# A two-number read of every eighth row of x, issued by ScalarE ahead of the conditions

## The chip, the core and the metric

One NeuronCore of one Trainium2 chip runs the whole kernel. The metric is the device time of one execution in microseconds (us). The kernel before takes 46.37 us, the median of 3 runs (46.32 to 46.39).

## The reference

x is float32, 64 samples of 64 channels by 512 positions. Each sample has a condition, an index into a table of 200 matrices of 64 by 64. The result adds to each sample its own product with its matrix:

```python
w = weights[conditions]
return x + jnp.einsum('bct,bcd->bdt', x, w)
```

The kernel adds the identity to each matrix, so that one product gives the sum of both terms.

## The kernel before

Two samples make a pair: 128 partitions (2 samples of 64 channels), 32 pairs, 512 positions. x in HBM is laid out as [128, 32, 512], so one row of it is 64 KB and every eighth row is 512 KB further on. The work goes in 8 turns of four pairs each (`TURNS`), 1 MB of x and 1 MB of output a turn.

SP (`on_sync`) issues the eight loads of x (L85) without a wait; each has a semaphore of its own. It then waits for the load of turn 6 (L87), and from there issues one store a turn (L91), each after ScalarE and VectorE have both copied their half of the turn out of PSUM; the last turn's store is cut in two (L95). At the end it waits for all stores (L96).

ScalarE (`on_scalar`) first issues the load of the conditions, 64 numbers, one row (L99). Its first work then loads an activation table and zeroes the corners of `w_diag` (L102). After that it waits for `w_ready`, copies matrices into the diagonal blocks of `w_diag` (L107) and the first half of each turn's products into `y_sb` (L111, L116).

VectorE (`on_vector`) waits for the conditions, computes two table rows for each condition (L161), which TensorE spreads over the 128 partitions with small matmuls (L130); VectorE turns them into integers (L164). GpSimd (`on_gpsimd`) then issues the indirect gather of 128 table rows of 8 KB, 1 MB in all (L122). When they have landed VectorE adds the identity (L170), transposes blocks of 32 by 32 (L173) and so makes `w_all` ready. It then copies matrices (L179) and the second half of each turn's products (L182, L186).

TensorE (`on_tensor`) waits for `w_ready`. In turns 0 to 3 it multiplies each sample of a pair by itself with 64 by 64 tiles (L147), in turns 4 to 7 a pair at a time with the 128 by 128 block-diagonal `w_diag` (L143). Two sets of PSUM tiles let a turn run while the one before is copied out.

Each queue is in program order. The order around the change is thus written by hand: SP's queue holds the loads of x, ScalarE's the conditions, GpSimd's the gather. All of these transfers are carried by the same 16 DMA engines. In the profile, queue q1 is SP's, q10 is ScalarE's and q0 GpSimd's.

Of the kernel before, what the change touches and what calls it, by code (L numbers as in the profile page):

```python
# [7 lines left out]
def conditioned_residual_kernel(nc: bass.Bass, x: bass.AP, conditions: bass.AP, table: bass.AP, out: bass.AP):  # L8
# [10 lines left out]
    fp32 = mybir.dt.float32  # L19
# [3 lines left out]
    P, PAIRS, T = x.shape  # L23
# [9 lines left out]
    with ctx:  # L33
        def sbuf(name, shape, dtype):
            return ctx.enter_context(nc.sbuf_tensor(name, shape, dtype))

        def semaphore(name):
            return ctx.enter_context(nc.semaphore(name))

        x_sb = sbuf("x_sb", [P, PAIRS, T], fp32)  # L40
        y_sb = sbuf("y_sb", [P, PAIRS, T], fp32)
        condition = sbuf("condition", [1, PAIR, Q], i32)

        row_along = sbuf("row_along", [1, PAIR, K, Q], fp32)
# [11 lines left out]
                   for s in range(SETS)]  # L56

        x_loaded = [semaphore(f"x_loaded{turn}") for turn in range(TURNS)]
        condition_loaded = semaphore("condition_loaded")
        one_set = semaphore("one_set")  # L60
        zero_set = semaphore("zero_set")
# [12 lines left out]
        def halves(h):  # L74
            return slice(h * C, (h + 1) * C)

        def pairs_of(turn):
            return slice(4 * turn, 4 * turn + 4)

        def round_of(turn, j):  # L80
            return slice(4 * turn + 2 * j, 4 * turn + 2 * j + 2)

        def on_sync(sp):
            for turn in range(TURNS):
                sp.dma_start(x_sb[:, pairs_of(turn), :], x[:, pairs_of(turn), :]).then_inc(x_loaded[turn], 16)  # L85

            sp.wait_ge(x_loaded[LAST - 1], 16)  # L87
            for turn in range(LAST):
                sp.wait_ge(moved_by_act, turn + 1)
                sp.wait_ge(moved_by_dve, turn + 1)  # L90
                sp.dma_start(out[:, pairs_of(turn), :], y_sb[:, pairs_of(turn), :]).then_inc(stored, 16)  # L91
            for j in range(2):
                sp.wait_ge(moved_by_act, TURNS + j)
                sp.wait_ge(moved_by_dve, TURNS + j)
                sp.dma_start(out[:, round_of(LAST, j), :], y_sb[:, round_of(LAST, j), :]).then_inc(stored, 16)  # L95
            sp.wait_ge(stored, 16 * (TURNS + 1))  # L96

        def on_scalar(act):
            act.dma_start(condition[:, :, :], conditions).then_inc(condition_loaded, 16)  # L99
            act.wait_ge(zero_set, 1)  # L100
            for h in range(PAIR):
                nc.scalar.copy(w_diag[halves(h), :, (1 - h) * D:(2 - h) * D],  # L102
                               zero[halves(h), :].unsqueeze(2).to_broadcast([C, PAIRS - 4 * TILED, D]))
            act.wait_ge(w_ready, 1)
            for turn in range(TURNS):
                if turn < TILED:
                    nc.scalar.copy(w_diag[halves(0), pairs_of(turn), 0:D],  # L107
                                   w_all[halves(0), :, pairs_of(TILED + turn)].rearrange("p d n -> p n d"))
                if turn < LAST:
                    act.wait_ge(multiplied, turn + 1)  # L110
                    nc.scalar.copy(y_sb[:, 4 * turn:4 * turn + 2, :], product[turn % SETS][0][:, :, :]  # L111
                                   ).then_inc(moved_by_act, 1)

            for j in range(2):
                act.wait_ge(multiplied, TURNS + j)
                nc.scalar.copy(y_sb[:, 4 * LAST + 2 * j, :], product[LAST % SETS][j][:, 0, :]).then_inc(moved_by_act, 1)  # L116
# [36 lines left out]
        def on_vector(dve):  # L153
# [30 lines left out]
            for j in range(2):  # L184
                dve.wait_ge(multiplied, TURNS + j)
                nc.vector.tensor_copy(y_sb[:, 4 * LAST + 2 * j + 1, :], product[LAST % SETS][j][:, 1, :]  # L186
                                      ).then_inc(moved_by_dve, 1)

        on_sync(nc.sync)
        on_scalar(nc.scalar)  # L190
        on_gpsimd(nc.gpsimd)
        on_tensor(nc.tensor)
# [30 lines left out]
```

## Time and profile before

| | before |
|---|---|
| median of 3 runs | 46.37 us |
| the profiled execution | 46.28 us |
| its span, first to last instruction | 45.0 us |
| HBM read, written | 9.44 MB, 8.39 MB |
| mean rate over the span | 396 GB/s |
| TensorE busy | 23.1 us |
| VectorE, ScalarE, GpSimd busy | 14.9, 13.9, 1.6 us |
| granted TensorE clock, mean | 0.977 of full speed |

All times in the rows count from the start of the span. The profiled execution is 1.28 us longer than its span, which is what lies around the first and last instruction. "Share" of the DMA is the mean busy share of the 16 engines; in narrow windows a packet counts where it starts, so shares over 1 occur there. Issuing a transfer is done by a queue (ACTq, SPq, POOLq) and doesn't count as busy time of the engine.

### The profile page before, as it was taken

To read this page: it belongs to the slowest core of one execution; us is meant where nothing else is said; L and a number is where in the kernel's file an instruction comes from. 1 tells how busy PE (TensorE), PEld (TensorE's weight loads), DVE (VectorE), ACT (ScalarE), POOL (GpSimd) and SP (SyncE) were. 2 spreads that over 40 slices of the span, in tenths; PEclk is the share of its full clock that TensorE was granted. 3 is DMA by queue.
4 is the path that set the end of the run, shared out by engine and by line. 5 is a ranking of instruction groups with operands and counts; after the bars stand their busy time and mean duration, and the time that the engine had idled before them with its cause. 6 is when DMAs were issued, how large, how long until landed. Compare 5 with 4: busy or idle time off the path is not lost.

```text
span 45.0 us, 294 instructions
## 1 busy us (share of the span) xinstructions
PE 23.1 (51%) x98; PEld 9.9 (22%) x98; DVE 14.9 (33%) x24; ACT 13.9 (31%) x16; POOL 1.6 (4%) x9
## 2 busy tenths in 40 slices
PE   0040000000000079999999999999999999200000
PEld 0040000000000034243463453443544433000000
DVE  1310000000019940069999900820720753600000
ACT  0899100000000050068988800800710733500000
POOL 4009000000000000000000000000000000000000
PEclk9999999999999999999999999999999999999955
DMA  0679999999999999999999999999999999999993
GB/s 0 124 299 423 423 423 430 430 423 437 423 423 430 430 423 437 423 423 430 408 437 423 423 437 423 415 444 415 423 437 415 430 430 423 423 430 426 383 415 146
DMA packets 2594, 17.83 MB, mean 396 GB/s; under 512 B 290, under 2 KB 290, under 8 KB 546
## 3 DMA queue, kind: packets, MB, share of 16 engines
q1 hardware_dynamic: 2448, 16.78, 89.9%
q0 software_dynamic: 144, 1.05, 5.5%
q10 hardware_dynamic: 2, 0.00, 0.0%
HBM read 9.44 MB, written 8.39 MB: 396 GB/s over the span
## 4 chain that ended last, share of the span: by engine, by line
PE 51%; DMA 24%; DVE 8%; issue 2%; DVEq 0%
PE product L143 31%; DMA gathered<-weights,table_row 22%; PE product L147 19%; DVE w_all L173 5%; DMA condition<-conditions 3%; DVE y_sb L186 2%; PE product L130 1%; DVE row_along L161 1%; DVE gathered L170 1%; DVE table_row L164 0%; DVEq L167 0%
## 5 line engine op out<-in xcount | busy, mean ns | idle before, releaser
L147 PE MATMUL product<-x_sb,w_all 64*64 64x512 f32 x64 | 8.6, 696 | 13.0 <-DVE w_all L173 13.0
L143 PE MATMUL product<-x_sb,w_diag 128*128 128x512 f32 x32 | 14.0, 595 | 0.0
L182 DVE COPY y_sb<-product 128x1024 f32<-128x1024 f32 x7 | 8.6, 1224 | 10.2 <-PE product L143 6.8
L111 ACT COPY y_sb<-product 128x1024 f32<-128x1024 f32 x7 | 7.1, 1012 | 10.9 <-PE product L143 7.4
L143 PEld LDWEIGHTS product<-x_sb,w_diag 128*128 128x128 f32 x32 | 6.0, 190 | 7.9 <-issue 7.9
L147 PEld LDWEIGHTS product<-x_sb,w_all 64*64 64x64 f32 x64 | 3.4, 206 | 17.5 <-DVE w_all L173 13.1
L107 ACT COPY w_diag<-w_all 64x256 f32<-64x256 f32 x4 | 2.6, 639 | 11.3 <-DVE w_all L173 11.3
L170 DVE TENSOR_TENSOR gathered<-gathered,piece 128x64 f32<-128x64 f32 x1 | 0.3, 268 | 10.2 <-DMA gathered<-weights,table_row 10.2
L173 DVE STREAM_TRANSPOSE w_all<-gathered 128x2048 f32<-128x2048 f32 x1 | 2.3, 2312 | 0.0
L102 ACT COPY w_diag<-zero 64x1024 f32<-64x1024 f32 x2 | 2.1, 1042 | 0.0
L186 DVE COPY y_sb<-product 128x512 f32<-128x512 f32 x2 | 1.4, 691 | 1.5 <-PE product L143 1.5
L130 PE MATMUL product<-one,row_along 1*128 1x1 f32 x2 | 0.6, 344 | 2.4 <-DVE row_along L161 2.4
L116 ACT COPY y_sb<-product 128x512 f32<-128x512 f32 x2 | 1.2, 585 | 1.8 <-PE product L143 1.8
L102 ACT ACT_TABLE_LOAD x1 | 1.3, 1283 | 1.3 <-PEq L201 1.3
L179 DVE COPY w_diag<-w_all 64x256 f32<-64x256 f32 x4 | 1.6, 400 | 0.1
L122 POOL DMA_INDIRECT gathered<-weights,table_row x1 | 1.1, 1068 | 2.1 <-DVE table_row L164 2.1
L130 PEld LDWEIGHTS product<-one,row_along 1*128 1x128 f32 x2 | 0.5, 308 | 2.4 <-issue 2.4
L161 DVE TENSOR_SCALAR row_along<-condition 1x64 f32<-1x64 int32 x2 | 0.3, 179 | 0.7 <-DMA condition<-conditions 0.7
L164 DVE CAST table_row<-product 128x1 int32<-128x1 f32 x1 | 0.2, 159 | 0.7 <-PE product L130 0.7
L120 POOL MEMSET piece<- 32x1 f32 x4 | 0.4, 91 | 0.5 <-POOLq L201 0.3
L154 DVE MEMSET zero<- 128x1 f32 x1 | 0.1, 59 | 0.8 <-PEq L201 0.8
L157 DVE MEMSET piece<- 32x1 f32 x4 | 0.2, 59 | 0.2
(5 smaller groups left out, 0.5 us busy)
## 6 DMA issues: line engine op xcount, KB each, us to landing
x_sb<-x SPq DMA_DIRECT2D x8, 1024.0 KB, 14.2
out<-y_sb SPq DMA_DIRECT2D x7, 1024.0 KB, 7.0
out<-y_sb SPq DMA_DIRECT2D x2, 512.0 KB, 5.8
condition<-conditions ACTq DMA_DIRECT2D x1, 0.2 KB
gathered<-weights,table_row POOLq DMA_INDIRECT x1, 9.8
```

The lines of the kernel that those rows point to most:

```text
L102: nc.scalar.copy(w_diag[halves(h), :, (1 - h) * D:(2 - h) * D], zero[halves(h), :].unsqueeze(2).to_broadcast([C, PAIRS - 4 * TILED, D]))
L107: nc.scalar.copy(w_diag[halves(0), pairs_of(turn), 0:D], w_all[halves(0), :, pairs_of(TILED + turn)].rearrange("p d n -> p n d"))
L111: nc.scalar.copy(y_sb[:, 4 * turn:4 * turn + 2, :], product[turn % SETS][0][:, :, :]).then_inc(moved_by_act, 1)
L116: nc.scalar.copy(y_sb[:, 4 * LAST + 2 * j, :], product[LAST % SETS][j][:, 0, :]).then_inc(moved_by_act, 1)
L122: nc.gpsimd.indirect_dma_start(gathered[:, :], None, table, bass.IndirectOffsetOnAxis(ap=table_row[:, 0:1], axis=0)).then_inc(w_gathered, 16)
L130: nc.tensor.matmul(product[0][0][:, 0, 0:1], row_along[:, :, :, :].rearrange("one h k n -> one (h k n)"), one[:, :], start=True, stop=True ...
L143: product_of = nc.tensor.matmul(product[turn % SETS][j][:, g, :], w_diag[:, n - 4 * TILED, :], x_sb[:, n, :], start=True, stop=True)
L147: product_of = nc.tensor.matmul(product[turn % SETS][h][halves(g), j, :], w_all[halves(h), :, n], x_sb[halves(h), n, :], start=True, stop= ...
L173: nc.vector.transpose(w_all[:, :, :], gathered[:, :].rearrange("p (d c) -> p d c", d=D)).then_inc(w_ready, 1)
L179: nc.vector.tensor_copy(w_diag[halves(1), pairs_of(turn), D:PAIR * D], w_all[halves(1), :, pairs_of(TILED + turn)].rearrange("p d n -> p n ...
L182: nc.vector.tensor_copy(y_sb[:, 4 * turn + 2:4 * turn + 4, :], product[turn % SETS][1][:, :, :]).then_inc(moved_by_dve, 1)
L186: nc.vector.tensor_copy(y_sb[:, 4 * LAST + 2 * j + 1, :], product[LAST % SETS][j][:, 1, :]).then_inc(moved_by_dve, 1)
```

## The change

A scratch of 16 partitions with two float32 numbers each is added. ScalarE's first instruction becomes a transfer of elements 0 and 1 of rows 0, 8, 16, ... 120 of x into it, 16 rows of 8 bytes; the load of the conditions follows on the same queue. SP waits for this transfer at its very end, after the last store is issued. Nothing reads the scratch.

```diff
+        touched = sbuf("touched", [P // 8, 1, 2], fp32)
...
+        rows_touched = semaphore("rows_touched")
...
                 sp.dma_start(out[:, round_of(LAST, j), :], y_sb[:, round_of(LAST, j), :]).then_inc(stored, 16)
+            sp.wait_ge(rows_touched, 16)
             sp.wait_ge(stored, 16 * (TURNS + 1))

         def on_scalar(act):
+
+            act.dma_start(touched[:, :, :], x.rearrange("(r e) n t -> r e n t", e=8)[:, 0, 0:1, 0:2]
+                          ).then_inc(rows_touched, 16)
             act.dma_start(condition[:, :, :], conditions).then_inc(condition_loaded, 16)
             act.wait_ge(zero_set, 1)
```

## Rows read from the trace of the kernel before

**Rows 1.** The page, part 2: tenths of busy time in 40 slices of the span.

```profile
PE   0040000000000079999999999999999999200000
...
DMA  0679999999999999999999999999999999999993
GB/s 0 124 299 423 423 423 430 430 423 437 423 423 430 430 423 437 423 423 430 408 437 423 423 437 423 415 444 415 423 437 415 430 430 423 423 430 426 383 415 146
```

**Rows 2.** The chain that ended last, in order of time: start, duration, what.

```profile
0.75 1.18 DMA condition<-conditions
...
1.96 0.30 DVE row_along L161 x2
...
2.39 0.57 PE product L130 x2
...
2.98 0.17 DVE table_row L164
...
3.42 9.78 DMA gathered<-weights,table_row
...
13.61 2.32 DVE w_all L173
...
15.97 8.63 PE product L147 x63
24.61 13.95 PE product L143 x32
...
38.58 0.69 DVE y_sb L186
```

**Rows 3.** Windows: stretch, its length, five engines busy, clock, DMA share, GB/s.

```profile
4.80:7.20 2.40, 0.00 (x0) 0.00 (x0) 0.00 (x0) 0.00 (x0) 0.00 (x0) 1.00 1.03 430
...
13.20:22.91 9.71, 6.94 (x52) 2.90 (x56) 6.22 (x7) 3.73 (x5) 0.00 (x0) 1.00 1.02 428
22.91:24.40 1.49, 1.49 (x16) 0.52 (x11) 1.43 (x2) 1.46 (x2) 0.00 (x0) 1.00 1.02 423
...
24.40:36.40 12.00, 12.00 (x32) 5.40 (x29) 5.11 (x5) 4.14 (x5) 0.00 (x0) 1.00 1.01 425
...
39.20:44.50 5.30, 0.00 (x0) 0.00 (x0) 0.07 (x1) 0.00 (x0) 0.00 (x0) 0.85 0.96 396
```

**Rows 4.** Timeline of the issuing queues, single issues: start, duration.

```profile
0.75 0.49 ACTq L99 DMA_DIRECT2D condition<-conditions  x1
...
0.76 0.38 SPq L85 DMA_DIRECT2D x_sb<-x  x1
...
1.19 0.43 SPq L85 DMA_DIRECT2D x_sb<-x  x1
...
33.01 0.33 SPq L91 DMA_DIRECT2D out<-y_sb  x1
...
36.44 0.33 SPq L91 DMA_DIRECT2D out<-y_sb  x1
...
37.62 2.05 SPq L95 DMA_DIRECT2D out<-y_sb  x2
...
39.34 0.33 SPq L95 DMA_DIRECT2D out<-y_sb  x1
```

**Rows 5.** The start: queues in 1.6:1.7, then in 1.7:1.8, then three windows.

```profile
q10 hardware_dynamic: 2, 0.00, 1.5%
...
q1 hardware_dynamic: 4, 0.03, 203.9%
...
1.78:4.80 3.02, 0.55 (x2) 0.50 (x2) 0.45 (x3) 2.86 (x3) 1.07 (x1) 1.00 0.98 355
...
2.20:2.40 0.20, 0.01 (x1) 0.04 (x1) 0.04 (x1) 0.20 (x1) 0.00 (x0) 1.00 0.15 41
2.40:2.60 0.20, 0.20 (x2) 0.20 (x2) 0.00 (x0) 0.19 (x2) 0.00 (x0) 1.00 0.31 123
```

**Rows 6.** Timeline of ScalarE up to 16 us.

```profile
1.28 1.28 ACT L102 ACT_TABLE_LOAD   x1 [1.28 <-PEq L201]
...
2.57 2.10 ACT L102 COPY w_diag<-zero 64x1024 f32<-64x1024 f32 x2
...
15.95 0.63 ACT L107 COPY w_diag<-w_all 64x256 f32<-64x256 f32 x1 [11.29 <-DVE w_all L173]
```

**Rows 7.** Waits of SP's queue: total us, times, longest.

```profile
SPq L96 <- DMA out<-y_sb: 5.3, 1, 5.3
```

**Rows 8.** Timeline of GpSimd, its indirect transfer.

```profile
3.42 1.07 POOL L122 DMA_INDIRECT gathered<-weights,table_row  x1 [2.15 <-DVE table_row L164]
```

**Rows 9.** DMA queues in 4.5:7.7, then 7.7:10, then 10:12.3: packets, MB, share.

```profile
q1 hardware_dynamic: 196, 1.34, 100.6%
...
q0 software_dynamic: 63, 0.52, 52.9%
q1 hardware_dynamic: 60, 0.49, 50.4%
...
q0 software_dynamic: 66, 0.53, 54.6%
q1 hardware_dynamic: 69, 0.44, 45.7%
```

## The prediction, made before the changed kernel was run

> **What bounds the kernel now.** I read the page first. The DMA engines are 9 tenths busy from the third slice to the last but one, and move 423 to 437 GB/s in nearly all of them [rows 1]; TensorE is busy for only 23 of 45 us. The chain of waits nevertheless runs through the conditions, the gather and TensorE, because the profile follows the last store back to the copy that released it [rows 2]. So two limits run side by side, and the question is which has room. From 4.8 us on the transfers go at 425 to 430 GB/s without a hole, and the last 5.30 us of them move 396 x 5.30 = 2.10 MB [rows 3], which is exactly the last two stores' worth (1 MB of turn 6, twice 0.5 MB of turn 7). So turn 6's store begins to flow at 39.2 us. It was issued at 36.44 [rows 4]. An issue needs 1.02 us to its first packet: x's first transfer is issued at 0.76, and its queue q1 is first seen moving in 1.70 to 1.80, at about 1.78 [rows 4, 5]. Its packets could have started at 37.46, so they waited 39.20 - 37.46 = 1.74 us behind older stores. Of the other stores, turn 5's was issued at 33.01 and takes 2.46 us to flow (1.05 MB at 425 GB/s), so it has 39.20 - 2.46 - 34.03 = 2.7 us of room, and turn 7's two have 39.20 + 2.46 - (37.62 + 1.02) = 3.0 and, for the last, 42.9 - (39.34 + 1.02) = 2.5 us. Turn 6 is the tightest: **everything from the conditions to the copies may slip by 1.74 us before a DMA engine runs dry; each further us is a us of time.** Conversely the only things that shorten the run are fewer bytes or an earlier or fuller start of the transfers.
>
> The start is not full: from 1.78 to 4.80 us only 355 GB/s x 3.02 us = 1.07 MB move [rows 5], which at 430 GB/s takes 2.49 us. So 0.53 us are lost there, nearly all before 2.8, where the engines show 41 to 123 GB/s in 2.2 to 2.6 [rows 5].
>
> **The change, part by part.**
>
> *The added issue on ScalarE.* The conditions' issue takes 0.49 us on ACT's queue, and SP's issues of the same form 0.38 to 0.43 when seen singly [rows 4, 6]. The touch is taken at 0.49, so the conditions are issued at 1.24 instead of 0.75. ACT's table load and its two fills of w_diag move along by 0.49, from an end at 4.67 to 5.16; w_all frees ACT's next copy only at 15.95, and 10.8 us of idle time cover it [rows 6]. Without that cover it would cost its 0.49.
>
> *The transfer itself.* It has 16 rows of 8 bytes, so some 16 data packets and up to 16 completions. The conditions' two packets filled 1.5% of 16 engines for 0.1 us, that is 24 ns on one engine [rows 5]. One such pair on each engine is 24 ns, ahead of x in time that is idle anyway: 0, or 0.02 if it comes into x's way.
>
> *The wait at SP's end.* The touch has landed long before; behind it stands only the wait for the stores, 5.3 us long [rows 7]. Cost 0; uncovered, one semaphore check, for which no row has a duration.
>
> *x's loads.* SP issues its first at the same moment as ACT (0.76 against 0.75), so they move past nothing in program order. The conditions' packets came at 1.6 to 1.7, x's first at 1.78 [rows 5]: ACT's first transfer is about 0.14 us ahead. If the slow start is the price of a first access to x's rows, the touch pays it 0.14 us earlier. Bounds: 0 (start unrelated, or the touch's packets no faster than x's own), 0.14 if x's packets still wait for the same accesses, 0.53 if 8 bytes open a region so much faster that nothing is left; below nothing -0.1 if both issues share what makes descriptors (SP's issues grew from 0.38 to 0.43 beside it). I take 0.1.
>
> *The conditions' landing, which is the term that matters.* They now reach the engines after x's packets instead of before them. Their issue ends at 1.24 + 0.49 = 1.73; before, it ended at 1.24 and the packet came at 1.64, 0.4 later. Lower bound: served at once, at 2.13, a delay of 0.49. Upper bound from the nearest row, the only transfer of another queue that is set behind x's: the gather's issue ends at 3.42 + 1.07 = 4.49 [rows 8], and up to 7.70 its queue q0 moves nothing, while q1 is 100% busy [rows 9]. That is 3.2 us, so the conditions' packet would come at 4.93, a delay of 3.3. In that wait are also steps of GpSimd's software queue, which ACT's has not. What the wait is for x's packets: at 1.73 each engine holds the eight packets that x's first transfer gives it (1,024 KB in 8 KB packets over 16 engines), and these are through at 4.80. If the conditions get in only ahead of the last one, they come at 4.80 - 0.31 (8 KB at 26.7 GB/s, a sixteenth of 427) = 4.49, and the delay is 4.49 - 1.64 = 2.85. I take 2.85: it is nearer to the gather's row than to an empty engine. All that follows is a chain with no slack of its own: two row_along, the matmuls, table_row, the gather, the diagonal, the transpose, PE at 15.97 [rows 2]. The gather keeps its 9.8 us, since q0 and q1 share alike once it flows (63 and 60 packets to 10.0 us, 66 and 69 after [rows 9]) and x's loads still flow then. PE starts at 18.8, the stores come 2.85 later, and 2.85 - 1.74 = 1.11 us reach the end.
>
> In that last stretch the rows show the two queues alternating in small steps. The Trainium skill (DMA: Bandwidth & Descriptors, Queues, rings and completion order) says that an engine drains a whole packet of several descriptors from one row's ring before it turns to the next, typically 9 to 17. By that rule the conditions wait for all eight of x's, +3.2 and an end at about 47.8; the equal counts in both halves of the gather do not show such blocks, so the sum above does not use it.
>
> **Sum.** Against the profiled execution's own 46.28 us (span 45.0 and 1.28 around it; 0.09 under the median of 46.37): +1.11 - 0.1 = +1.0, thus 47.3, and 47.4 against the median. What a measurement of this kernel can tell from no change is about 0.2%, 0.09 us.
>
> **Rivals.**
> A. *Hidden, no change.* The conditions get in between x's first packets (delay 0.5 to 1.7, under the room of 1.74) and the slow start stays as it is. For it: the packet-by-packet sharing [rows 9]. Against: the 3.2 us. Time 46.3 to 46.45.
> B. *Faster.* The conditions are as quick as in A, and the touch opens x's regions. 46.37 - 0.14 to 46.37 - 0.53: 45.85 to 46.25, about 46.15. For it: the slow first packets are seen only at the start; the first stores after 22.9, to an output not yet touched, show no dip (428 and 423 GB/s [rows 3]), which speaks against a first-access price for every region.
> C. *The conditions wait for x's second transfer too*, issued at 1.19 and so ahead of them: it is through at about 7.2, a delay of 5.5, +3.8, 50.1. For it: the gather began only as x's second transfer was through.
> D. *The change does nothing it says*: x opens its own rows 0.14 us behind and the start is as slow, as in A, but with the conditions late: the forecast without its 0.1, 47.5; it is in the forecast.
> The point of decision between forecast and A is a delay of 1.74 us, four or five of x's packets on one engine.
>
> **Chances.** Forecast (slower, delay 1.8 to 3.3, with or without the 0.1): 0.47. A 0.18, B 0.29, C 0.04; a small loss of 0.1 to 0.3 us with quick conditions, from an x start that the touch pushes back, 0.02. Slower 0.53, same 0.18, faster 0.29. Both signs hold much of it: the forecast's own range is 46.6 (delay 2.0) to 48.0 (3.3 and no gain). The range reaches down into B, to 46.0, and up to 48.1.
>
> **What would show it.** Conditions: the wait of row_along ends at 4.8 instead of 1.96 (2.5 to 3.6 in A or B). PE's first product at 18.8; turn 6's store issued at 39.3; a hole of about 1 us in the DMA share before it. In 1.78 to 4.80 the rate stays near 355 GB/s; in B it rises over 390. The forecast is wrong if row_along starts before 3.7, or if the transfers show no hole and the span shrinks.

## The result, and the profile after

The changed kernel takes 48.55 us (median of 6 runs, 47.96 to 51.16) against 46.34 us for the kernel before beside it: a ratio of 1.041, 95% interval 1.035 to 1.046. The ratios here compare only runs in the faster of two states, into which executions of either kernel fall; of these six that leaves four, with a median of 48.26 us against 46.32. It is slower, as forecast, but by 1.9 us (2.2 in the profiled pair) where 1.0 was said, and above the range, which ended at 48.1. The profiled execution took 48.45 us, its span 47.2 us, against 46.28 and 45.0.

Part 2 of the page, the kernel after, 40 slices of the span:

```profile
PE   0000040000000000099999999999999999992000
...
DMA  0679999999999999999981999999999999689995
GB/s 0 118 320 424 424 424 424 424 438 424 431 417 438 410 438 424 410 424 424 431 341 42 403 445 431 389 403 445 438 389 417 424 445 403 264 341 438 382 414 205
```

Against [rows 1] the row of the DMA engines has two new holes: one at slice 22 (42 GB/s), where before the first store already flowed, and one at slices 35 and 36 (264 and 341 GB/s), ahead of turn 6's store. The first three slices, where the touch was to help, have not become fuller (118 and 320 GB/s, before 124 and 299).

The chain that ended last, kernel after: start, duration, what.

```profile
1.19 4.21 DMA condition<-conditions
...
5.42 0.29 DVE row_along L168 x2
...
6.88 10.45 DMA gathered<-weights,table_row
...
17.73 2.32 DVE w_all L180
...
20.10 8.74 PE product L154 x58
28.84 13.95 PE product L150 x32
...
42.81 0.69 DVE y_sb L193
```

Line by line against [rows 2]: the conditions are issued 0.44 us later (1.19 against 0.75), but row_along starts 3.46 us later (5.42 against 1.96). The gather takes 10.45 us instead of 9.78, another 0.67. PE starts 4.13 us later, and the last copy 4.23 us later.

DMA queues of the kernel after, in 1.7:2.15, then in 2.15:3.6, then in 4.8:4.9 (packets, MB, share of 16 engines):

```profile
q1 hardware_dynamic: 13, 0.11, 142.3%
...
q1 hardware_dynamic: 52, 0.43, 77.3%
q10 hardware_dynamic: 32, 0.00, 1.2%
...
q1 hardware_dynamic: 10, 0.05, 132.1%
q10 hardware_dynamic: 2, 0.00, 1.7%
```

ScalarE's q10 has 34 packets now: 32 of the touch and 2 of the conditions. The touch was not ahead of x at all: 13 packets of x started by 2.15 us, and the touch's 32 came only after that. The conditions' two came in 4.8 to 4.9, where x's first load is through, instead of 1.6 to 1.7 [rows 5].

Windows of the kernel after (as [rows 3]), and the first store and turn 6's store in the timeline of SP's queue:

```profile
1.78:4.80 3.02, 0.00 (x0) 0.00 (x0) 0.00 (x0) 3.00 (x3) 0.00 (x0) 1.00 0.99 347
24.64:25.90 1.26, 1.26 (x16) 0.63 (x12) 1.18 (x3) 1.09 (x3) 0.00 (x0) 1.00 0.02 7
...
40.68:41.70 1.02, 1.02 (x3) 0.38 (x2) 0.60 (x1) 0.59 (x1) 0.00 (x0) 1.00 0.47 193
...
25.06 0.35 SPq L94 DMA_DIRECT2D out<-y_sb  x1
...
40.68 0.33 SPq L94 DMA_DIRECT2D out<-y_sb  x1
```

The start moves 347 GB/s, before 355 [rows 5]: nothing was opened. The engines stand still for 1.26 us after the last load, because turn 0's copies are not yet there (VectorE's ends at 24.96, the store is issued at 25.06, before at 22.91). Turn 6's store is issued at 40.68 instead of 36.44, and in the 1.02 us until its packets can start the engines move only 193 GB/s.

### The profile page after: what moved, and what is told of

Its sections match the earlier page's. It is cut to its first block, busy times and chain, and to the rows that moved or that the text cites. A ratio compares the mean times of both kernels' runs of the same rounds, so it can differ in the third digit from the quotient of the medians.

```text
span 47.2 us, 295 instructions
## 1 busy us (share of the span) xinstructions
PE 23.2 (49%) x98; PEld 10.0 (21%) x98; DVE 14.9 (32%) x24; ACT 13.8 (29%) x16; POOL 1.7 (4%) x9
## 4 chain that ended last, share of the span: by engine, by line
PE 49%; DMA 31%; DVE 8%; issue 1%; ACTq 1%; DVEq 0%
PE product L150 30%; DMA gathered<-weights,table_row 22%; PE product L154 19%; DMA condition<-conditions 9%; DVE w_all L180 5%; DVE y_sb L193 1%; PE product L137 1%; ACTq L104 1%; DVE row_along L168 1%; DVE gathered L177 1%; DVE table_row L171 0%; DVEq L174 0%
## 6 DMA issues: line engine op xcount, KB each, us to landing
gathered<-weights,table_row POOLq DMA_INDIRECT x1, 10.5
```

## Experiments

The columns of windows and queues in this section are those already explained. On the four chips used for these runs the time around the span lay anywhere between 1.3 and 2.4 us, for the kernel before too; so spans are compared beside the times. All readings of packets and starts come from one profiled execution of each kernel.

**The touch behind the conditions.**

```diff
-            act.dma_start(touched[:, :, :], ...).then_inc(rows_touched, 16)
             act.dma_start(condition[:, :, :], conditions).then_inc(condition_loaded, 16)
+            act.dma_start(touched[:, :, :], ...).then_inc(rows_touched, 16)
```

> The touch follows the conditions on ScalarE's queue; nothing else differs from the changed kernel. Theory (all the loss is the conditions falling behind x's first eight packets on their engine): the conditions land at 1.9 us as before, row_along starts at 1.96, PE at 16.0, and the time is that of before, 46.3 us within 0.2. Rival 1 (the touch itself costs transfer time, or upsets x's first transfer): some of the 2.2 us stay, 46.8 or more. Rival 2 (the touch opens x's rows and the start becomes fuller): under 46.2.

row_along started at 1.98 and PE at 15.92, as before: the conditions' lateness is gone with the order of the two transfers. The times, 46.27 to 47.59 against 46.72 to 47.30, could not tell half a us, so the same kernel was timed again:

> The kernel with the touch behind the conditions once more, in more rounds, since its first comparison did not resolve 0.5 us. Theory (the touch costs and gives nothing by itself): within 0.2 us of the kernel before. Rival 1: slower by 0.3 us or more, from a touch that stands behind x's first load. Rival 2: faster.

Ratio 1.0014, interval 0.9991 to 1.0038; the spans behind it were 45.0 to 45.3 against 44.9 to 45.2. The touch by itself costs nothing that can be measured, and gives nothing. ScalarE's queue in 4.9:5.8, the profile of this second timing:

```profile
q10 hardware_dynamic: 30, 0.00, 1.8%
```

Issued right behind the conditions, 30 of its 32 packets came in this stretch and the last two by 6.5, all of them after x's first load was through: here it is the touch that waits, and nobody waits for it.

**Another first transfer.** The touch is replaced by a read of the 256 bytes of the conditions themselves into a scratch of that size; the rest is the same.

```diff
-            act.dma_start(touched[:, :, :], x...[:, 0, 0:1, 0:2]).then_inc(rows_touched, 16)
+            act.dma_start(touched[:, :, :], conditions).then_inc(rows_touched, 16)
```

> In place of the touch ScalarE first reads the conditions into a scratch, one row, 256 bytes, and reads nothing of x. Theory (an issue of about 0.45 us ahead is enough, whatever it reads): the second read lands at 4.8 to 5.4, PE starts at 19.5 to 20.3 and the time is 47.8 to 48.6. Rival (the 16 small packets of the touch or their rows of x are what holds the conditions up): the conditions land at 2.3 to 2.6, 0.45 late, and the time is 46.3.

Ratio 1.039 (1.030 to 1.049). The conditions' packets came in 4.9 to 5.0, row_along started at 5.47 and PE at 19.98. Three of the four times (48.44 to 49.16) lie above the forecast's 48.6, on a chip where the kernel before took 46.72 to 47.30; the spans were 46.8 to 47.9 against 44.9 to 45.1. It makes no difference what is read, nor in how many packets.

**No first transfer, only the lateness.** The kernel before with one wait:

```diff
+            act.wait_ge(pieces_set, 2 * (P // Q))
             act.dma_start(condition[:, :, :], conditions).then_inc(condition_loaded, 16)
```

> The kernel before, with one wait ahead of the conditions' issue (for the eight pieces, set at 1.28 us), so they are issued at about 1.3 instead of 0.75, and no transfer stands ahead of them. Theory (a late issue alone does it): packet at 4.8 to 5.2, behind x's first eight, row_along at 5.3 to 5.6, time 48.0 to 48.6. Rival (it needs another transfer ahead on ScalarE's queue): packet at 2.2, time as before.

The chain that ended last, this kernel:

```profile
1.31 4.00 DMA condition<-conditions
...
5.33 0.29 DVE row_along L162 x2
...
6.79 10.33 DMA gathered<-weights,table_row
```

The same 4 us from issue to landing, with nothing ahead on ScalarE's queue. The fastest of its four runs took 48.33 us, span 47.0 (the kernel before beside it 44.8 to 45.0 in all runs but one of 46.2). The step that costs is the late issue beside x's loads, and nothing of the touch.

**Later still.** A memset of 1,024 columns on VectorE, with a semaphore that ScalarE waits for ahead of the conditions:

```diff
+            act.wait_ge(filled, 1)
             act.dma_start(condition[:, :, :], conditions).then_inc(condition_loaded, 16)
...
+            nc.vector.memset(unused[:, :], 0.0).then_inc(filled, 1)
```

> The same, with the issue held by a memset of 1,024 columns on VectorE, to about 1.9 to 2.4 us, when three of x's loads are issued. If the wait is for what an engine has read ahead, about eight packets: packet 0.9 + 2.5 us after the start of the issue, 5.3 to 5.8. If it is for every load issued ahead: x's second is through at 7.2 and its third at 9.7, so the packet comes at 7.2 or later.

The issue started at 2.50 us, later than meant. The queues in 0:6.3, then in 6.3:6.4, this kernel, and the start of row_along:

```profile
q1 hardware_dynamic: 225, 1.71, 71.4%
...
q1 hardware_dynamic: 10, 0.08, 193.1%
q10 hardware_dynamic: 1, 0.00, 1.1%
...
7.01 0.29 DVE row_along L165 x2
```

The packet came 3.8 to 3.9 us after the issue began. That is 2.9 to 3.0 more than the 0.9 of an empty engine (0.75 to 1.64), or nine to ten packets of 0.31; the forecast said eight. x's second load was issued more than a us before. Of the 2.10 MB of its first two loads 1.71 MB had begun when the packet came, so the second was not waited for to its end. So the wait isn't for all loads issued ahead. It has the length of eight to ten of x's packets; that the engine has read these ahead is the reading that fits, and no row shows it directly.

**Issued behind the fill of w_diag in program order.**

```diff
-            act.dma_start(condition[:, :, :], conditions).then_inc(condition_loaded, 16)
...
+                if h == 0:
+                    act.dma_start(condition[:, :, :], conditions).then_inc(condition_loaded, 16)
```

> The kernel before, with the conditions issued after ScalarE's first fill of w_diag, at 3.1 us instead of 0.75, so that they reach the engines at about 4.0 in the middle of x's first load, with six more loads issued. If an engine has read ahead some eight packets of whatever queue: packet at 4.0 + 8 x 0.31 = 6.5, row_along at 6.9. If it is every load issued ahead of it: x's first three or four, 9.6 us or more. If the queues simply alternate and the wait of the changed kernel belongs to the start alone: 4.4. The time follows from row_along's lateness less 1.74: 6.5 gives 4.9 - 1.74 = 3.2 more.

This missed its aim: the issue did not wait for the fill. It began while the table load was running, only 0.17 us late. Timeline of this kernel:

```profile
0.75 1.28 ACT L101 ACT_TABLE_LOAD   x1 [0.75 <-PEq L202]
...
0.92 0.49 ACTq L104 DMA_DIRECT2D condition<-conditions  x1
...
3.50 0.28 DVE L162 TENSOR_SCALAR row_along<-condition 1x64 f32<-1x64 int32 x2 [2.23 <-DMA condition<-conditions]
```

It gives a point in between: 0.17 us late in the issue, packet in 2.8 to 2.9, row_along 1.54 us late. The span stayed at 45.0 in the profile, as the room of 1.74 us has it (45.6 in the other run); the times (46.88 and 47.37) resolve nothing. The question that it was to answer, a late issue in the middle of the stream, is answered by the run with the memset alone.

**x's first load in two halves.** The changed kernel with eight packets of 4 KB an engine first:

```diff
-                sp.dma_start(x_sb[:, pairs_of(turn), :], x[:, pairs_of(turn), :]).then_inc(x_loaded[turn], 16)
+                for pairs in ([slice(0, 2), slice(2, 4)] if turn == 0 else [pairs_of(turn)]):
+                    sp.dma_start(x_sb[:, pairs, :], x[:, pairs, :]).then_inc(x_loaded[turn], 16)
...
-                pe.wait_ge(x_loaded[turn], 16)
+                pe.wait_ge(x_loaded[turn], 32 if turn == 0 else 16)
```

> The changed kernel with x's first load cut in two of 512 KB, so that each engine gets eight packets of 4 KB (1.2 us of transfer) before the second half's eight. Theory by whole load (the conditions wait until the load issued ahead of them is through on their engine, and the second half is issued at the same time as they are): packet at 3.5 to 3.8 instead of 5.0, row_along at 3.9 to 4.2, end 1.2 us earlier, 47.0 to 47.3. Rival (they wait for a fixed number of bytes, or until the queue is read in some 3 us): row_along still at 5.2 to 5.5, time 48.3.

The conditions' packets came in 3.7 to 3.8, row_along at 4.30. Half the bytes ahead of them, and they are 1.1 us earlier: the wait is for x's packets, and for a number of them rather than of bytes, since these are eight again, of half the size. One run took 47.06 us, span 45.8, as forecast; the other, the profiled one, 48.89 and 47.6.

**The gather on empty engines.** The kernel before, with x's loads from the second on held until the gather has landed.

```diff
+                if turn == 1:
+                    sp.wait_ge(w_gathered, 16)
                 sp.dma_start(x_sb[:, pairs_of(turn), :], x[:, pairs_of(turn), :]).then_inc(x_loaded[turn], 16)
```

> The kernel before, with x's loads from the second on held until the gather has landed: the gather meets engines that are idle from 4.8 us on. It measures the gather's 3.2 us between the end of its issue (4.49) and its first packet. If the wait is for x's packets that the engines had read ahead: first packet at 5.0 to 5.5, and the gather through 2.5 us later, landing at 8.0. If it is the software queue's own latency: first packet at 7.7 as before, landing at 10.5. The total time is longer by the lost transfer time and is not what is asked.

Queues in 4.5:5.1, then in 5.1:5.3, this kernel:

```profile
q1 hardware_dynamic: 25, 0.09, 36.7%
...
q0 software_dynamic: 8, 0.07, 256.8%
q1 hardware_dynamic: 2, 0.00, 0.6%
```

The gather's first packet came at about 5.2, 0.7 us after its issue's end, and not at 7.7. Of the 3.2 us that the prediction read in [rows 9], 2.5 were x's packets ahead, eight of them, and 0.7 its own way. Landing was at 9.1, not 8.0, so that its 1 MB takes 3.9 us even alone, where 2.5 were expected; part of this is a slow start.

This run also shows two more starts on engines that stood still: the gather's at 5.18, and x's second load's at 10.09, after 1.2 us without a packet. Their first 3.02 us, this kernel, and beside them the first us of the stores in the changed kernel, which begin at 25.90 on engines that stood still as well:

```profile
5.18:8.20 3.02, 0.00 (x0) 0.00 (x0) 0.00 (x0) 0.00 (x0) 0.00 (x0) 1.00 0.99 320
10.09:13.11 3.02, 1.22 (x8) 0.59 (x12) 2.13 (x2) 0.63 (x1) 0.00 (x0) 1.00 1.02 345
...
25.90:26.90 1.00, 1.00 (x12) 0.36 (x8) 0.97 (x2) 1.00 (x2) 0.00 (x0) 1.00 1.08 451
```

Both starts of reads are as slow as x's first (355 GB/s [rows 5]), and the start of the stores isn't. In the kernel before the same second load of x follows the first without a break and runs at 430 GB/s [rows 3]. So the slow start belongs to reads that begin on idle engines, three times of three here, and not to the first access to x.

**The touch really ahead.** SP's loads are held until 1.3 us, in the kernel before and in the changed one.

```diff
         def on_sync(sp):
+            sp.wait_ge(pieces_set, 2 * (P // Q))
             for turn in range(TURNS):
```

> The kernel before, with SP's loads held for 0.55 us by a wait for the pieces. Control for the next one. x's first packet at 2.3; every later transfer 0.55 later, time 46.9. Theory of the slow start (first packets of all engines at once are slow, whenever they come): the first 3 us of transfer still lose 0.5 us.

> The changed kernel with the same hold: the touch is now some 0.6 us ahead of x's first packets, and the conditions (issued at 1.2) come ahead of them too, at 2.1. Theory: no conditions' wait for x, PE 0.45 later than before (16.4), time as x_held, 46.9. Rival (touching opens x's rows where it really comes first): x's first packets take 0.31 us instead of 0.4 to 1.0 and the time is up to 0.5 us under x_held, 46.4.

The first 3.02 us of x's transfers, first without, then with the touch:

```profile
2.32:5.34 3.02, 0.55 (x2) 0.50 (x2) 0.16 (x1) 2.31 (x3) 1.07 (x1) 1.00 0.97 353
```

```profile
2.31:5.33 3.02, 0.55 (x2) 0.49 (x2) 0.44 (x3) 2.77 (x3) 1.07 (x1) 1.00 0.98 339
```

All 32 packets of the touch lay in 1.7 to 2.0 here, 0.3 us or more ahead of x's first at 2.3. x's start moved 339 GB/s, without it 353: rows touched beforehand are not read faster. The spans, 45.7 with the touch and 45.4 to 45.7 without, say the same, and so do the times: 47.0 and 46.7 to 47.0 us, as forecast for no effect. With the hold the conditions came ahead of x again and row_along started at 2.43.

**The room, measured by itself.** The kernel before with an additional transpose of the gathered rows into a scratch, of 1,024 and of 2,560 columns; nothing changes at the start.

```diff
             dve.wait_ge(identity_added, 1)
+            nc.vector.transpose(unused[:, 0:1024], gathered[:, 0:1024])
```

The version with 2,560 columns has two such lines, of 2,048 and of 512.

> The kernel before, with one more transpose of 1,024 columns on VectorE (half of the 2.31 us one, 1.16 us) between the identity and the real transpose: everything from w_all on comes 1.16 us later and no transfer at the start changes. Theory (there are 1.74 us of room before turn 6's store): time within 0.2 of before. Rival (there is no room, PE's chain sets the end): +1.16.

> The same with 2,560 columns, 2.9 us later. Theory: +2.9 - 1.74 = +1.15, a hole of about 1.1 us in the transfers ahead of turn 6's store. Rival (no room): +2.9. Rival (the loss comes from the reordering of the transfers at the start, not from PE's lateness): +0.

With 1,024 columns PE started at 17.27, 1.30 late, and the ratio is 1.0003 (0.9955 to 1.0050); the transfers show no hole:

```profile
24.00:41.00 17.00, 16.65 (x60) 7.00 (x52) 8.47 (x10) 7.36 (x10) 0.00 (x0) 1.00 1.01 424
```

With 2,560 columns PE started at 18.73, 2.76 late, and the hole ahead of turn 6's store is there, with the start of the transfers unchanged:

```profile
40.30:41.50 1.20, 1.20 (x4) 0.57 (x3) 0.71 (x2) 0.50 (x2) 0.00 (x0) 1.00 0.24 96
```

Its spans were 45.8, 46.6, 46.7 and 47.1, that is 0.8 to 2.1 over 45.0 where 1.0 follows from 2.76 - 1.74. The profiled execution explains its own: TensorE's first 64 products took 10.08 us (8.63 before), so the last copy began 4.19 late. Over the profiled executions, by the start of the last copy (before: 38.58):

| kernel | last copy late | less 1.74 | span over 45.0 |
|---|---|---|---|
| conditions behind the fill | 1.60 | 0 | 0.0 |
| 1,024 columns | 2.11 | 0.37 | 0.2 |
| x's first load in two | 2.77 | 1.03 | 2.6 (other run 0.8) |
| conditions twice | 3.92 | 2.18 | 1.8 |
| 2,560 columns | 4.19 | 2.45 | 2.1 |
| the change | 4.23 | 2.49 | 2.2 |
| conditions waited | 4.46 | 2.72 | 3.3 (other run 2.0) |
| conditions late | 6.08 | 4.34 | 4.0 |

Two profiled executions stand out above the line, and another run of each (0.8 and 2.0) does not. The others lie at the forecast or 0.2 to 0.4 under it, so the room is nearer 2.0 than 1.74 us. The last copy's lateness holds more than the delay put in: TensorE's first 64 products took 8.6 to 10.1 us over these runs, with the same work, for a reason that no run isolates. With the touch second (second timing) the last copy was 1.26 late by this alone, inside the room, and the span 45.2.

No version beat the kernel before. The touch second is as fast; the room says that an earlier landing of the conditions can't gain, and the start did not respond to the touch.

## Why the prediction was wrong in size and right in direction

Two terms of the sum failed in size, the conditions' landing (2.85 us, measured 3.46) and the gather, whose length was taken as unchanged (measured 0.67 longer). The mechanism, a small load caught behind x's first one and a room that it overruns, was right.

*The bound.* Right: the transfers set the end and the chain of the conditions had some 1.74 us of room. Two kernels that change only w_all's lateness show it: one at the room's edge, where the time did not change, and one beyond, with the hole and spans 0.8 to 2.1 longer. The prediction did not say that the first store could come too late: turn 0's store had room as well, of about 2.6 us (24.4 less its copy's end at 20.73 and 1.02), and this was used up too (the hole at 24.64). It did not add to the loss, since turn 6's delay is larger and is counted from the same end.

*The conditions behind x's first load: the step that carried the forecast.* Its mechanism was right and is shown from three sides: it needs no touch, it shrinks with x's first load, and it is gone when the conditions are issued first. The size was set at 2.85 and measured 3.46, for two reasons. "If the conditions get in only ahead of the last one" failed: they come behind all eight, at 4.8 to 4.9 instead of 4.49, 0.36 more. And from packet to row_along took 0.57 us against 0.3 before, 0.25 more. The rule of the Trainium skill (DMA: Bandwidth & Descriptors, Queues, rings and completion order) that an engine drains a whole packet of descriptors before it turns to another row gave +3.2 for this step, and the packet did come 3.2 later (4.8 to 4.9 against 1.64), nearer than my own 2.85. In the run with the memset the wait was nine to ten packets, which the rule would allow as well. But where gather and x flow together the engines change queue after every packet of 8 KB. The kernel with 2,560 columns shows it best, queues in 7.83:8.13, 8.13:8.43 and 8.43:8.73, each one packet long:

```profile
q0 software_dynamic: 13, 0.11, 83.7%
q1 hardware_dynamic: 3, 0.02, 19.3%
...
q1 hardware_dynamic: 13, 0.11, 83.7%
q0 software_dynamic: 3, 0.02, 19.3%
...
q0 software_dynamic: 13, 0.11, 84.2%
q1 hardware_dynamic: 3, 0.02, 19.3%
```

So the rule came near the number, but blocks of 9 or more are not seen in the flow, and the measurement decides: what waits for eight to ten packets is only the first packet of a queue that comes late.

*"The gather keeps its 9.8 us."* Wrong, and the larger of the misses: it took 10.45. Between its issue and its first packet nothing changed (from 7.95 to 11.1 only q1 moved, 3.2 us again). The flow was longer: the last 8 KB packet started 5.1 us after the first, before 4.6 (16.2 and 11.1; 12.3 and 7.7), and the landing came 1.1 instead of 0.9 us after that. Over the runs in which x's loads flow beside it the gather took from 9.6 to 10.5 us, 10.3 also with x held and the conditions on time, and 9.9 with the latest conditions of all; so lateness alone does not explain it. What makes the flow longer was not isolated and stays open. I had given this term no range at all, and that is why the range ended at 48.1.

*The start.* 0.1 was taken as gained; nothing was. The premise "ACT's first transfer is about 0.14 us ahead" came from the conditions' one row and fell for 16 rows: the touch came behind x's first packets. And the held pair shows that it would have gained nothing if it had been ahead. That refutes rival B's price, 0.14 to 0.53. Its argument that slow first packets are seen only at the start does not hold either: they come back wherever reads begin on idle engines. (The row that the prediction cites for the first stores, 22.91 to 24.40, still holds loads; the stores flow from 24.40, at 425 GB/s [rows 3], so what it concludes of them stands.)

*The other steps.* The DMA digits of [rows 1] reach 9 in the fourth slice and not in the third; nothing hangs on it. The touch's issue was taken at 0.49 and lasted 0.41, and the conditions' came 0.44 late. Its packets and the wait at SP's end cost nothing, as said (the touch second: 1.0014).

*Sum again, with what was measured.* 3.46 + 0.67 + 0.10 (last copy against PE's start) = 4.23, less 1.74 is 2.49; the span grew by 2.2. Against the forecast's +1.0: 0.61 from the conditions, 0.67 from the gather, 0.1 from the copy, 0.1 from the start, less 0.3 of room underrated. This sum is of the profiled pair.

*Rivals.* A (hidden) needed the conditions served between x's first packets. That happens when their issue is 0.17 us late (packet in 2.8 to 2.9, span unchanged), not when it is 0.44 late. C (behind x's second load too) did not come about at 0.44 or 0.56, nor at 1.75, where the packet came in the middle of that load. The sign was right by the mechanism, not by luck.

## What to carry to other kernels

A tiny transfer that starts a dependent chain has to be the first on its queue and issued no later than the first large load: 0.44 us of delay in the issue became 3.5 us in the landing, since it then stood behind all eight packets of x that each DMA engine had first. If it can't be first, make the load that it meets small, or hold that load: holding x's loads for 0.55 us put the landing back to 2.4 us at the price of that hold. And before an engine's chain is shortened or lengthened, work out from store issues and rates how much room it has; here 1.7 to 2.0 us of lateness were free and every further us cost one.

## What had not been expected

- The step is steep: issue of the conditions at 0.75, 0.92, 1.19 and 2.50 us, packet at 1.6, 2.8, 4.8 and 6.3. The first 0.17 us of delay cost 1.2, the next 0.27 cost 2.0, and another 0.12 (issue at 1.31) nothing: the packet came at 4.8 again.
- A transfer of 16 rows, issued at the same moment as x's load, has its packets behind x's first ones (after 2.15, x from 1.78), while one of a single row came ahead (1.6 to 1.7). With x held, where nothing is in its way, the 16 rows' first packet came after 1.7 too.
- A transfer's issue that stands behind an activation on ScalarE's queue in the program began during the table load (0.92, table load 0.75 to 2.03), before the activation had run (2.04): here its place behind compute, without a wait, did not hold the issue back.
- The slow start of x's transfers (339 to 355 GB/s over the first 3 us) is the same with x 0.55 us later and with its rows touched beforehand, and comes back in the middle of a run (320 and 345) when reads begin on idle engines. What in such a start is slow is open.
